# End of a graph layer: the last tile's sums ahead of two tiles' products, and its rows stored in halves

## The reference, cut to what matters

```python
def _rgcn_layer(X, W, root, bias, gamma, beta, src, dst, etype, inv_deg):
    h = jnp.einsum('ni,rio->rno', X, W)
    msg = h[etype, src] * inv_deg[:, None]
    agg = jax.ops.segment_sum(msg, dst, num_segments=X.shape[0])
    out = agg + X @ root + bias
    mu = jnp.mean(out, axis=-1, keepdims=True)
    var = jnp.mean(jnp.square(out - mu), axis=-1, keepdims=True)
    out = (out - mu) * jax.lax.rsqrt(var + EPS) * gamma + beta
    out = jax.nn.elu(out)
    return out + X
```

## Time and profile before

| what | value |
|---|---|
| median of 3 runs | 2796.46 us (2795.09 to 2799.65) |
| the profiled execution, its own time | 2799.68 us |
| its span in the trace | 2797.9 us |
| granted TensorE clock, mean | 0.82 of 2.4 GHz |
| PE busy | 2142.3 us (77%) |
| DVE busy | 1675.8 us (60%) |
| POOL busy | 1515.5 us (54%) |
| ACT busy | 371.0 us (13%) |
| last gather to first gather of the next layer | 30.5, 31.8 and 31.3 us at the three layer ends |

### The profile page before, as it was taken

The page is one execution under the profiler, slowest core; times in us unless marked ns, Lnnn a source line. Parts: engine busy times, 40 slices in busy tenths (PEclk is TensorE's granted clock), DMA queues, the critical chain, the costliest instruction groups (busy, mean ns, idle before and its releaser), DMA issues.

```text
span 2797.9 us, 45858 instructions
## 1 busy us (share of the span) xinstructions
PE 2142.3 (77%) x7689; PEld 1298.2 (46%) x7690; DVE 1675.8 (60%) x6024; ACT 371.0 (13%) x765; POOL 1515.5 (54%) x1591
## 2 busy tenths in 40 slices
PE   1667976777888889898888898887888787765554
PEld 0445444666444455434445563444555434444443
DVE  3988259787445566434456672345567435567776
ACT  0554320232000111100011110000111100000000
POOL 1000033000777777477777756777777477777750
PEclk9878975899778999856889995679899856788776
DMA  4000241000344444333444443344444433333430
GB/s 154 1 0 0 112 155 36 0 0 11 105 120 128 135 144 149 97 105 113 121 134 142 143 127 97 105 120 128 135 143 150 143 105 109 108 111 112 115 87 9
DMA packets 103478, 280.48 MB, mean 100 GB/s; under 512 B 27932, under 2 KB 39306, under 8 KB 103054
## 3 DMA queue, kind: packets, MB, share of 16 engines
q0 software_dynamic: 75264, 205.62, 25.7%
q10 hardware_dynamic: 18198, 62.19, 5.9%
q1 hardware_dynamic: 9848, 10.82, 1.2%
HBM read 219.61 MB, written 58.91 MB: 100 GB/s over the span
## 4 chain that ended last, share of the span: by engine, by line
PE 38%; DVE 18%; issue 14%; DMA 12%; POOL 11%; DVEq 3%; ACT 1%; POOLq 1%; SPq 1%; ACTq 0%
PE acc L458 21%; POOL ring L270 11%; DMA ring<-h_rows,idx 11%; PE hp L367 6%; PE pw L367 6%; DVE S L887 2%; PE acc L449 2%; PE pw L343 1%; DVE hot_s L860 1%; DVE ring L737 1%; DVE hot_n L860 1%; DVE S L910 1%; DVE rs L806 1%; POOLq L181 1%; DVE rsv L803 1%
## 5 line engine op out<-in xcount | busy, mean ns | idle before, releaser
L270 POOL DMA_INDIRECT ring<-h_rows,idx x1568 | 1507.9, 962 | 1193.7 <-issue 904.0
L458 PE MATMUL acc<-ring,S 128*128 x3712 | 1248.7, 472 | 326.6 <-DVE S L910 158.4
L458 PEld LDWEIGHTS acc<-ring,S 128*128 128x128 f32 x3712 | 750.8, 223 | 801.4 <-issue 726.6
L910 DVE TENSOR_SCALAR S<-iota,ecol 128x128 f32<-128x128 f32 x1856 | 605.9, 367 | 792.2 <-PE acc L458 708.4
L367 PE MATMUL hp<-wts,XT 128*128 (+1 forms) x416 | 214.6, 664 | 22.4 <-ACT XT L493 22.4
L367 PE MATMUL pw<-wts,XT 128*128 (+1 forms) x384 | 198.2, 664 | 20.3 <-ACT XT L493 20.3
L551 ACT ACTIVATE work<-work 128x256 f32<-128x256 f32 x100 | 41.7, 417 | 980.7 <-DVE work L940 970.3
L860 DVE TENSOR_TENSOR hot_s<-iota,place 128x400 bf16<-128x400 f32 x196 | 111.8, 571 | 99.9 <-PE acc L410 84.8
L449 PE MATMUL acc<-wts,XT 128*128 (+1 forms) x400 | 121.1, 431 | 41.3 <-issue 36.6
L367 PEld LDWEIGHTS hp<-wts,XT 128*128 128x128 f32 x416 | 84.2, 213 | 122.3 <-issue 122.3
L493 ACT ACTIVATE XT<-tr 128x256 f32<-128x256 f32 x100 | 38.3, 383 | 693.2 <-PE tr L356 683.9
(11 more groups left out here) (204 smaller groups left out, 1407.5 us busy)
## 6 DMA issues: line engine op xcount, KB each, us to landing
h_rows<-hst ACTq DMA_DIRECT2D x100, 512.0 KB, 2.9
ring<-h_rows,idx POOLq DMA_INDIRECT x1568, 2.8
wts<-weights SPq DMA_DIRECT2D x32, 128.0 KB, 3.0
x_rows<-X ACTq DMA_DIRECT2D x1, 3200.0 KB, 10.1
wts<-x_rows ACTq DMA_DIRECT2D x1, 3200.0 KB, 11.6
X<-x SPq DMA_DIRECT2D x1, 3072.0 KB
out<-work ACTq DMA_DIRECT2D x24, 128.0 KB
wts<-roots SPq DMA_DIRECT2D x8, 128.0 KB, 3.0
```

Source lines behind the costliest of these rows:

```text
L270: pool.indirect_dma_start(ring[:, k, :], None, h_gather, bass.IndirectOffsetOnAxis(ap=idx[:, g * J + j:g * J + j + 1], axis=0)).then_inc(l ...
L458: nc.tensor.matmul(accs[t % 2][:, 0:D], S[:, at * J + j, :], ring[:, bass.ds((c + j) % SLOTS, 1), :].rearrange("p a d -> p (a d)"), start= ...
L910: v.tensor_scalar(S[:, at * J + j, :], iota[:, t * P:(t + 1) * P], dst_c[:, bass.ds(c + j, 1)], inv_c[:, bass.ds(c + j, 1)], ALU.is_equal, ...
```

## The change

On PE, sums(24) move ahead of products(22): the order at the end of a layer becomes sums of 23, sums of 24, then products of 22, 23 and 24. On DVE, `weigh_rest` of tile 24 moves ahead of norm(23), since sums(24) must not wait for it. ACT's sequence is as it was, but `products_out` of tile 24 stores each bank as soon as it is copied: two stores of 256 KB instead of one of 512 KB, and the counts on `h_stored0` rise by one per layer.

```diff
             def gathers(l, h_gather):
-                pool.wait_ge(s["h_stored0"], (l + 1) * (16 * (NT // 2 + 1)))
+                pool.wait_ge(s["h_stored0"], (l + 1) * (16 * (NT // 2 + 2)))
                 pool.wait_ge(s["h_stored1"], (l + 1) * (16 * (NT // 2)))
...
                 for t in range(NT):
                     aggregate(l, t, lm, lg)
-                    if t > 0:
-                        e = l * NT + (t + NT - 1)
-                        turn(e, t - 1)
-                        node_products(e, t - 1, l + 1, e if t == 1 else e - 1)
-                e = l * NT + (2 * NT - 1)
-                turn(e, NT - 1)
-                node_products(e, NT - 1, l + 1, e - 1)
+                    if t == NT - 2:
+                        continue
+                    for done in ((t - 2, t - 1, t) if t == NT - 1 else (t - 1,)):
+                        if done < 0:
+                            continue
+                        e = l * NT + (done + NT)
+                        turn(e, done)
+                        node_products(e, done, l + 1, e if done == 0 else e - 1)
...
                     nc.scalar.activation(hst[:, half, b * 512:(b + 1) * 512], hps[half][b], ACT.Copy).then_inc(s["h_out"], 1)
-                act.wait_ge(s["h_out"], e * 2 + 2)
-                act.dma_start(h_rows[layer][t * P:(t + 1) * P, :], hst[:, half, :]).then_inc(s[f"h_stored{half}"], 16)
+                    if t == NT - 1:
+                        act.wait_ge(s["h_out"], e * 2 + (b + 1))
+                        act.dma_start(h_rows[layer][t * P:(t + 1) * P, b * 512:(b + 1) * 512],
+                                      hst[:, half, b * 512:(b + 1) * 512]).then_inc(s[f"h_stored{half}"], 16)
+                if t < NT - 1:
+                    act.wait_ge(s["h_out"], e * 2 + 2)
+                    act.dma_start(h_rows[layer][t * P:(t + 1) * P, :], hst[:, half, :]).then_inc(s[f"h_stored{half}"], 16)
...
                     weigh_first(t, visits, lm)
+                    if t == NT - 1:
+                        weigh_rest(t, visits, lm)
                     if t > 0:
                         layer_norm_elu(l, t - 1, lm + tile_end(t - 1), features(t - 1))
-                    weigh_rest(t, visits, lm)
+                    if t < NT - 1:
+                        weigh_rest(t, visits, lm)
                 layer_norm_elu(l, NT - 1, lm + tile_end(NT - 1), features(NT - 1))
```

More of the change, by code:

```diff
@@ L556, in _ @@
                     transposed(l * NT + (t + NT), t)
-                    products_out(l * NT + (t + NT), t, (l + 1) % 2, (l + 1) * (NT // 2 + 1 - t % 2) + t // 2)
+                    products_out(l * NT + (t + NT), t, (l + 1) % 2, (l + 1) * (NT // 2 + 2 - 2 * (t % 2)) + t // 2)
             act.wait_ge(s["h_mm"], L * NT * 2)
```

## The result

The changed kernel takes 2810.43 us in the median (2807.82 to 2812.49, 5 runs), the kernel before 2796.46: a ratio of 1.0045, 95% interval 1.0031 to 1.0060, so 14 us slower. The profiled execution's span is 2810.4 us against 2797.9.

What follows compares the result with a forecast made beforehand. POOL, issuing 392 gathers in 493 us per layer, paces the kernel, so only its idle time at three layer ends changes. 3 x (4.16 - 0.65) + 3.1 = +13.6 us on the median 2796.46 gives 2810, range 2802 to 2818.

Steps and rivals of the forecast that it cites:

- PE's loads: Before tile 24's root product, four table loads directly behind sums(23) leave PE idle 1.95 us per layer end.
- ACT: Exp(23), like exp(24), waits behind the second copy of the products before: one more 2.00 us PE hole per layer end.
- One sign: At each layer end, exp(23) and exp(24) would both be released by the copy on ACT.
- The stretch: Layer end from the end of sums(23) to the last copy: 26.21 us against 22.05, +4.16 us each.
- Norm(23) on DVE: At the layer end, starts about 1146, minimum ready about 1150.7: early enough to cost nothing.
- Norm(24) on DVE: Begins with turn(23), needs 4.63 us of 5.71 until ACT is free; nothing added, at most 0.1 us for its table entry.
- The store: Last tile's store in halves lands sooner: -0.65 us per layer end, bounds 0 and -1.3.
- The clock: One more hole per layer end lets the granted clock fall: +1.0 us each, +3.1 for three, bounds -3.1 and +7.1.
- Hidden loads: Rival: the sequencer runs ahead, so PE's table loads cost nothing at three layer ends; +7.8, 2804.3 us, chance 0.13.
- products without holes: Rival: norms 23 and 24 run under products 22 and 23 at layer ends; -5.9, 2790.6 us, chance 0.05.
- Little happens: Rival: clock falls at no hole and store gains 1.3 us per end (+5.5, 2802), or loads hidden plus one; chance 0.15.
- the faster rival: The rival of products without holes at the layer ends: 2790.6 us, chance 0.05.

Runs made afterwards that it cites:

- the order alone: The changed kernel with the last tile stored whole, as in the kernel before: 1.0055 of the time of the kernel before.
- the two mended kernels: Kernel before with halved last store and exp(24) between copies: 0.9979; changed kernel with PE's loads ahead and exp(23), exp(24) between copies: 0.9995.

## Why the prediction was right

- **What bounds the kernel.** Right: 493 us from first to last gather in the layers behind a layer end (492.3 to 494.4 in all nine profiles), and what the change is seen to do lies in the gaps.
- **PE's loads.** Forecast 1.95 us, measured 2.06 to 2.12. Rows 7 were the right place to look: from the start of the last eight matmuls of sums(23) to the next root product it takes 4.05 to 4.18 us at all twelve ends with the exposed loads. (The two equal values of rows 7 are less constant than they look: the thirteen such places between 2577 and 2769 us of that trace have 3.91 to 4.29, 4.02 on average.) Taking the loads away took the idle time away, so what was drawn from the queue rule of the Trainium skill (TensorE: Matmul & The Clock Gate, the table of specifications and step 5 of Part 2), loads hidden under queued matmuls, did not come about behind sums. Behind the eight matmuls of products(22) it did: there L449 starts at 1144.66, as they end.
- **ACT.** Right by its mechanism and its size: 2.04 us, twice. Exp(23) behind the copy shows it, and moving it ahead shrank the hole to 0.54. One sign did not come: exp(24) was to be released by the copy, and the rows of the first profile put it down to DVE's minimum at all three ends. The hole is the same, as ACT was free only 0.2 us after that minimum.
- **The stretch.** Forecast 26.21 us at full clock, measured 26.33 and 26.29.
- **Norm(23) on DVE.** Its start was forecast 3.9 us after the root product of sums(24) (1142.1 to 1146). It came 5.66 us after it at full clock (1142.06 to 1147.72 with the order alone), as the last four matrices of tile 24 were begun only 3.5 us after that product. As forecast this cost nothing in the changed kernel: its minimum was ready 1.55 us before exp(23) could begin. It is what is left before turn(23) once the exponential is moved ahead.
- **Norm(24) on DVE.** Forecast to cost nothing, with 1.1 us to spare before its table entry. It cost nothing, with 0.2 us to spare at ends with slow sums(24) and without alike, as the table entry took 0.94 us.
- **The store.** Forecast -0.65 us per end. Whole stores landed 3.00 us after issue on average (six, 2.61 to 3.53), halves after 2.47 (21, 2.00 to 3.17): -0.53.
- **The clock.** This term, +3.1 us, was right in sign and wrong in place and size. I had priced falls only at the holes before the turns. But it fell behind the hole at the loads as well: in sums(24) and their root product, at all six ends of the two profiles of the changed kernel, 1.7 us each time (7.99 to 8.00 us, against 6.30 with the order alone), which the sum did not contain. Where that hole was gone, it did not fall there once. Behind the holes before the turns it fell once in six in the first profile and four times in six in the second. Against the 3.1 us that the kernel before lost itself, the term was +4.9 us in the first profile and +11.1 in the second; with the order alone it was -1.6.
- **The total.** 2810 forecast, 2810.4 measured. That close it is luck: the gaps of the profiled execution grew by 18.2 us and not by 13.6, and the times outside them happened to be low. Of the 4.6 us more, the clock has nearly 2 and the store 1.1 (three landings gained 0.8 in this profile, not 1.95); 1.2 lie between the last gather and the end of sums(23), and 0.3 in the stretch.
- **The rivals.** Hidden loads and products without holes both fell by the idle times in the profile. "Little happens" fell with the interval. How far an engine's order can be mended was the sound part of the faster rival: once exponentials and loads are moved too, the new order comes to the time of before, though not below it.

## What to carry to other kernels

When a step moves on one engine, look at what the other engines still have in front of it: here products moved behind sums on PE, and ACT's unchanged sequence turned that into a hole, since an exponential that had waited for no copy now stood behind copies that came late. Four register loads that cost nothing behind the matmuls of products(22) cost some 2.1 us here behind sums whose products each wait for a matrix. In a stretch where nothing else is left to do, find the chain that must follow itself (here sum, norm, exponential, turn, products, store) and shorten that; moving the work around it gained nothing, and taking one copy out of the exponential's way, together with the store in halves, gained 0.2%.

## What was not expected of the hardware

The granted clock fell to 0.50, the 1.2 GHz level, behind idle times of about 2 us in some cases and not in others of the same kernel. Behind the 2.04 us before a turn it fell in 15 of 33 cases over all profiles, and behind the 2.06 to 2.13 us at the loads in 9 of 12: at all three ends of both profiles of the changed kernel and of the one with the early exponential, at none with the order alone, though PE had done the same work before. Behind the idle times of 1.20 to 1.25 us of the two mended kernels it fell in none of six, and in sums(24) without the hole at the loads in none of 15. A fall cost 1.4 to 1.7 us in most cases, but 2.8 to 3.0 in three. What decides between the executions stays open; no run here was made to settle it.
